# Attention of a macaron block: which engine normalises the first two batches, and the order of copies and exponentials in the first

## The reference, cut to what matters

```python
x = L0_attn_x                                   # (8, 1024, 128) fp32
x = x + 0.5 * _L0_ffn_ref(_layernorm(x), ...)   # feed-forward block with 16 routed experts
x = x + _L0_attn_ref(_layernorm(x), Qw, Kw, Vw) # causal attention, one head, per batch
x = x + 0.5 * _L0_ffn_ref(_layernorm(x), ...)   # the feed-forward block again

def _layernorm(x): return (x - mean) / sqrt(var + 1e-5)      # over the 128 features
def _L0_attn_ref(x, Qw, Kw, Vw):
    scores = (x @ Qw) @ (x @ Kw).T / sqrt(128) + causal_mask
    return softmax(scores) @ (x @ Vw)
```

## Time and profile before

| | us |
|---|---|
| median of 3 runs | 685.28 |
| lowest, highest | 681.53, 686.0 |
| time of the profiled execution | 686.61 |
| its span | 684.8 |
| PE busy | 640.4 (94%) |
| DVE busy | 559.1 (82%) |
| ACT busy | 549.7 (80%) |
| POOL busy | 521.7 (76%) |

### The profile page before, as it was taken

One profiled execution on the slowest core, in us unless ns is written; L12 is line 12 of the kernel. 1 busy time (PEld: TensorE's weight loads), 2 busy tenths in 40 slices (PEclk: granted clock), 3 DMA queues, 4 the chain that ended last, 5 costly groups with the idle time before them and its releaser, 6 DMA issues.

```text
span 684.8 us, 15211 instructions
## 1 busy us (share of the span) xinstructions
PE 640.4 (94%) x3395; PEld 493.8 (72%) x3395; DVE 559.1 (82%) x2576; ACT 549.7 (80%) x1171; POOL 521.7 (76%) x411
## 2 busy tenths in 40 slices
PE   4689999999999997699998998999999999999997
PEld 3457777777777765578776886777777777777775
DVE  5888989989899897767767768779889889898863
ACT  3478879898888874778887786769888898988975
POOL 3378889899998885665655546558899998999975
PEclk9699999999999999999999999999999999999999
DMA  9866677865777650334544435886867878768782
GB/s 245 194 139 128 140 160 151 167 130 129 161 158 165 134 124 1 59 74 76 96 81 78 74 76 96 162 161 123 171 143 159 176 170 174 160 142 187 167 172 76
DMA packets 107801, 92.05 MB, mean 134 GB/s; under 512 B 59488, under 2 KB 73456, under 8 KB 107760
## 3 DMA queue, kind: packets, MB, share of 16 engines
q1 hardware_dynamic: 105552, 91.00, 63.6%
q10 hardware_dynamic: 2208, 0.59, 0.4%
HBM read 72.70 MB, written 5.24 MB: 114 GB/s over the span
## 4 chain that ended last, share of the span: by engine, by line
PE 69%; DVE 13%; ACT 6%; issue 6%; DMA 3%; POOL 2%; SPq 0%; POOLq 0%; ACTq 0%; DVEq 0%
PE psum L1373 18%; PE psum L1374 17%; PE psum L1375 17%; PE psum L1446 3%; DVE w_raw L1246 3%; DMA wb<-scratch 2%; PE psum L1404 2%; PE psum L1458 2%; DVE zn L1272 1%; PE psum L1420 1%; DVE s_sb L1100 1%; PE psum L1412 1%; PE psum L1610 1%; ACT s_sb L759 1%; PE psum L1612 1%
## 5 line engine op out<-in xcount | busy, mean ns | idle before, releaser
L452 POOL TENSOR_TENSOR shared_r<-shared,shared_r 128x512 fp32r<-128x512 f32 x256 | 326.6, 1298 | 57.7 <-ACT shared L642 55.1
L1100 DVE SCALAR_TENSOR_TENSOR s_sb<-psum,wb 128x512 f32<-128x512 f32 x256 | 175.6, 687 | 47.4 <-DMA wb<-scratch 22.4
L641 ACT ACTIVATE shared_r<-s_sb 128x512 fp32r<-128x512 f32 x256 | 160.0, 625 | 46.3 <-DVE s_sb L1100 43.0
L642 ACT ACTIVATE shared<-s_sb 128x512 f32<-128x512 f32 x288 | 177.6, 619 | 20.0 <-DVE s_sb L1100 20.0
L1373 PE MATMUL psum<-x_hi,w_hi 128*128 128x512 f32 x288 | 126.3, 439 | 1.2 <-issue 0.9
L1373 PE MATMUL psum<-shared_r,w_hi 128*128 128x512 f32 x256 | 115.6, 452 | 1.2 <-POOL shared_r L452 1.0
L1375 PE MATMUL psum<-x_hi,w_lo 128*128 128x512 f32 x288 | 114.2, 396 | 0.0
L1374 PE MATMUL psum<-x_lo,w_hi 128*128 128x512 f32 x288 | 114.0, 396 | 0.0
L1374 PE MATMUL psum<-shared_r,w_hi 128*128 128x512 f32 x256 | 101.7, 397 | 0.0
L1375 PE MATMUL psum<-shared_r,w_lo 128*128 128x512 f32 x256 | 101.0, 395 | 0.0
L544 POOL TENSOR_TENSOR shared<-s_sb,shared 128x1024 f16<-128x1024 f32 (+3 forms) x32 | 56.7, 1771 | 44.3 <-ACT shared L572 44.3
(11 more groups left out here) (170 smaller groups left out, 1372.3 us busy)
## 6 DMA issues: line engine op xcount, KB each, us to landing
wb<-scratch SPq DMA_DIRECT2D x128, 512.0 KB, 7.9
out<-x_sb SPq DMA_DIRECT2D x16, 256.0 KB, 9.9
x_sb<-in_L_attn_x SPq DMA_DIRECT2D x4, 256.0 KB, 6.2
scratch<-wT SPq DMA_DIRECT2D x32, 32.0 KB, 1.9
w_raw<-in_L_ffn_W ACTq DMA_DIRECT2D x1, 512.0 KB, 6.0
w_raw<-in_L_ffn_W SPq DMA_DIRECT2D x1, 512.0 KB, 6.6
wb<-shared SPq DMA_TRANSPOSE x32, 4.1
w_raw<-in_L_ffn_Ws ACTq DMA_DIRECT2D x1, 64.0 KB, 8.7
```

Of the source, the lines that this page charges most:

```text
L452: nc.gpsimd.tensor_tensor(g_lo[:, j % RING, :], g_f[:, j % RING, :], g_hi[:, j % RING, :].bitcast(F32), ALU.subtract).then_inc(F.glo_done, 1)
L641: nc.scalar.activation(g_hi[:, j % RING, :], s_sb[:, j % RING, :], ACT.Square)
L642: nc.scalar.activation(g_f[:, j % RING, :], s_sb[:, j % RING, :], ACT.Square).then_inc(F.sq_done, 1)
L1100: ins = nc.vector.scalar_tensor_tensor(s_, h_, 0.0, wb[:, u, c, :], ALU.max, ALU.mult)
```

## The change: what it does

The diff has three parts.

1. DVE's `normalise` is gone. ACT normalises batches 0 and 1 too, two tiles a step: batch 0 at k = 4 to 7 (half 1 first), batch 1 at k = 14 to 17 (half 0 first). ACT needs the bias, so DVE makes `shift(0)` at k = 4 and `shift(1)` at k = 13; the second waits until batch 0 is normalised, since `a_shift` is one buffer.
2. DVE's statistics move: `stats(1, 1)` from k = 4 to 5, `stats(2, 0)` stays at k = 13, `stats(2, 1)` from k = 15 to 14, `mean(2)` from slot 1 of batch 0 to k = 17, and `stats(3, ...)` from slots 1 and 4 of batch 0 to slots 3 and 5.
3. In batch 0 alone, ACT does `exp(0, 0)` and `exp(0, 2)` ahead of the two `z_hi_copy` of batch 1, not behind them. DVE does `z_lo_part(1, 0)` and the last group's residual in slot 1, behind `row_max(0, 1)`, not in slot 0.

```diff
--- before.py
+++ after.py
@@ -772,18 +772,23 @@
                     sc.wait_ge(A.tp_done, HQ * b + SOON.index(t) + 1)
                     copy(pT[:, 0:t + 1, q0:q0 + P], tp_ps[:, 0:(t + 1) * P].rearrange("p (k q) -> p k q", q=P)).then_inc(A.pT_done, 1)
 
-                def normalise(b, half):
-                    sc.wait_ge(A.shift_done, b - 1)
+                def normalise(b, half, tiles=range(HQ)):
+                    sc.wait_ge(A.shift_done, b + 1)
                     tokens_free(sc, b, half)
-                    for t in range(half * HQ, (half + 1) * HQ):
+                    for t in (half * HQ + n for n in tiles):
                         ins = nc.scalar.activation(zn(b, half)[:, t % HQ, :], x_sb[:, b * QT + t, :], ACT.Identity, bias=a_shift[:, t:t + 1],
                                                    scale=a_rstd[:, b % UN, t:t + 1])
-                    ins.then_inc(A.zn_done[half], 1)
+                    if tiles[-1] == HQ - 1:
+                        ins.then_inc(A.zn_done[half], 1)
 
                 def begin(k):
 
                     if k == 3:
                         nc.scalar.activation(warm[:], neg_half[:], ACT.Exp)
+                    if k in (4, 5, 6, 7):
+                        normalise(0, (7 - k) // 2, range(k % 2 * 2, k % 2 * 2 + 2))
+                    if k in (14, 15, 16, 17):
+                        normalise(1, (k - 14) // 2, range(k % 2 * 2, k % 2 * 2 + 2))
                     if k == 8:
                         z_hi_copy(0, 1, misc_ps)
                     if k == 11:
@@ -806,9 +811,11 @@
                                 uT_copy(b - 1, 1)
                             if b > 0 and s == 6:
                                 uT_copy(b - 1, 0)
-                            if b + 1 < B and s in (0, 2):
+                            if b + 1 < B and s in (0, 2) and b > 0:
                                 z_hi_copy(b + 1, s // 2, prep_ps)
                             exp(b, s)
+                            if b == 0 and s in (0, 2):
+                                z_hi_copy(1, s // 2, prep_ps)
                             if s in (5, 6):
                                 pT_copy(b, SOON[s - 5])
                             if b + 1 < B and s in (4, 6):
@@ -1264,15 +1271,6 @@
                     nc.vector.scalar_tensor_tensor(a_shift, a_mv[b % UN][:, :, 0], -1.0, a_rstd[:, b % UN], ALU.mult,
                                                    ALU.mult).then_inc(A.shift_done, 1)
 
-                def normalise(b, half):
-                    v.wait_ge(A.rstd_done, b + 1)
-                    tokens_free(v, b, half)
-                    for t in range(HQ):
-                        tile = half * HQ + t
-                        ins = nc.vector.tensor_scalar(zn(b, half)[:, t, :], x_sb[:, b * QT + tile, :],
-                                                      a_mv[b % UN][:, tile, 0:1], a_rstd[:, b % UN, tile:tile + 1], ALU.subtract, ALU.mult)
-                    ins.then_inc(A.zn_done[half], 1)
-
                 def finish(b, half):
 
                     v.wait_ge(A.exp_done, QT * b + QT - half)
@@ -1294,42 +1292,42 @@
                         stats(0, 1)
                     if k == 2:
                         mean(0)
-                    if k in (3, 4):
-                        stats(1, k - 3)
-                    if k == 5:
-                        normalise(0, 1)
+                    if k == 4:
+                        shift(0)
+                    if k in (3, 5):
+                        stats(1, (k - 3) // 2)
                     if k == 6:
                         mean(1)
-                    if k == 7:
-                        normalise(0, 0)
                     if k == 9:
                         z_lo_part(0, 1, misc_ps)
-                    if k == 10:
-                        normalise(1, 0)
                     if k == 12:
                         z_lo_part(0, 0, u_ps)
-                        normalise(1, 1)
+                    if k == 13:
+                        shift(1)
+                        stats(2, 0)
                     if k == 14:
                         q_lo_part(0, 1, misc_ps)
-                    if k in (13, 15):
-                        stats(2, (k - 13) // 2)
+                        stats(2, 1)
                     if k == 16:
                         q_lo_part(0, 0, u_ps)
+                    if k == 17:
+                        mean(2)
 
                 def run():
                     for b in range(B):
                         for s in range(QT):
                             row_max(b, s)
-                            if b == 0 and s == 0:
+                            if b == 0 and s == 1:
+                                z_lo_part(1, 0, prep_ps)
                                 close_ffn()
                                 v.wait_ge(FF[0].res_done, NG)
-                            if b + 1 < B and s in (0, 2):
+                            if b + 1 < B and s in (0, 2) and (b, s) != (0, 0):
                                 z_lo_part(b + 1, s // 2, prep_ps)
                             if b + 1 < B and s in (5, 7):
                                 q_lo_part(b + 1, (7 - s) // 2, prep_ps)
-                            if b + 2 < B and s == 1:
+                            if 0 < b < B - 2 and s == 1:
                                 mean(b + 2)
-                            if b + 3 < B and s in (1, 4):
+                            if b + 3 < B and s in ((1, 4) if b > 0 else (3, 5)):
                                 stats(b + 3, s // 4)
                             if b + 2 < B and s == 3:
                                 shift(b + 2)
```

## The result

| | before | changed |
|---|---|---|
| median of 11 runs, us | 685.68 | 678.7 |
| lowest, highest | 681.2, 687.84 | 676.38, 679.64 |
| span of the profiled execution | 684.8 | 676.9 |
| mean granted clock | 0.982 | 0.997 |

The ratio is 0.9915, 95% interval 0.9896 to 0.9935: 5.8 us less of 685 (4.5 to 7.1); the two medians alone stand 7.0 apart. The forecast was 678.5, in a range of 675.3 to 682.8. The gain is just short of 1%, on the side that had the larger chance.

What follows compares the result with a forecast made beforehand. DVE's normalising was taken to hold PE before the first score. Gains of 6.4 us by the first row maximum and 7.4 by the fifth, taken as 6.8, bring 685.28 to 678.5 us; range 675.3 to 682.8.

Steps and rivals of the forecast that it cites:

- Who held PE: Before the first score, DVE's four groups of normalising instructions hold PE: about 9.6 us, 5.4 at the median, the rest blocking.
- ACT's run: From 249.14 us ACT does four pairs of squares and eight normalising instructions; zn's halves are ready at 252.9 and 256.4.
- First score: Batch 0's first score on PE starts at 266.1 us instead of 271.37, without a pause, taking 1.5 us instead of 2.7.
- First row maximum: Batch 0's first row maximum on DVE starts at 268.05 us instead of 274.44, 6.4 us gained; `mean(2)` costs 0.4.
- Fifth row maximum: In batch 0, the fifth maximum's exponential starts at 278.25 us instead of 285.69: 7.4 us gained, an extra 1.0.
- Moved whole behind it: From 285.69 us the rest of batch 0 keeps its length and all behind moves with it; gain taken 6.8 us.
- Rival B: PE gaps in batch 0 bring one or two more low-clock spells of 1.2 us: gain 4.4, 680.9 us; chance 0.22.
- Rival C: ACT bounds batch 0; late z copies delay low parts and row maxima; 2.5 to 4 us left, 682; chance 0.16.
- D: Nothing reaches the end because batch 1 starts on another wait (transposing transfers, PE's products): 685 us; chance 0.04.
- E: Moving 16 normalising instructions to ACT costs 0.8 us engine time and takes nothing off the path: 686.1 us; chance 0.02.
- F: PE waits for batch 0's zn at step 8 and runs the tail at low clock: 5 us slower, 690.3; chance 0.04.
- A: The forecast itself, for the whole kernel: gain of 5.8 to 8 us, 677 to 679.5 us; chance 0.52.

Runs made afterwards that it cites:

- the strided kernel: The kernel before, with DVE's normalising instructions reading every second value of two neighbouring tiles; ratio 0.9991 (0.9967 to 1.0014), last gate at 18.51 us.

## Why the prediction was right

- **Who held PE.** DVE, by its L1272. Shown both ways: with the normalising moved to ACT and nothing else the last gate moves from 19.02 to 13.59, and put back as unused work from 13.59 to 19.25.
- **ACT's run.** Forecast 249.14 to 252.9 and 256.4 for the two halves of zn, which is 3.8 and 7.3 behind the anchor. Measured 3.72 (250.60 + 0.86) and 7.35. Steps of streaming instructions, not their durations, were the right price for ACT. For DVE the prediction took durations: L1272 has 0.338 us of duration, but 0.26 from start to start where nothing holds it, so 16 of them are about 4.4 us and not 5.4, more of the 9.6 was blocking than it said, and the move adds about 2 us of plain engine time (0.385 against 0.26), not 0.8.
- **First score.** Forecast 16.96, measured 17.05; without a pause and at full clock.
- **First row maximum.** Forecast 18.91, measured 19.37, a gain of 5.9 instead of 6.4. The missing 0.5 is there already at the last gate (13.25 forecast, 263.0 less a gate of 0.61; 13.59 measured) and the square behind it, and it reaches the low part of the second q whole. The score was ready only 0.16 late, so `mean(2)` cost 0.65 (19.37 against 18.72), not 0.4.
- **Fifth row maximum.** Forecast 7.4 us gained at its exponential, measured 6.66 (36.55 to 29.89). The extra of batch 0's order was put at 1.0 on the way from the first to the fifth; it is 0.7 there (5.93 to 6.66), of which by the estimate above about 0.5 is the order and the rest the tail of the spell that before had at C. Against it stand the 0.65 of `mean(2)`, so the new order as a whole brought about nothing.
- **Moved whole behind it.** D to F: 12.03 before, 11.99 changed. The sum taken, 6.8, stands against 6.7 at F and 5.8 (4.5 to 7.1) in the ratio of the runs. That the forecast time is within 0.2 us of the median is partly luck: the runs of one kernel spread by 3 us and more, and the median of before moved by 0.4 with more runs.
- **Rival B** was half there: the clock fell at the end of batch 0, but it had fallen there before too, so it took nothing from the gain; a spell there is 1.6 us, not 1.2. **Rival C**: DVE's low parts did wait for the late copies (1.16 and 1.66 us idle), but it did not eat the gain. Filling the first wait with `mean(2)` gave 0.65 us at C, moving the second low part behind the fourth maximum 0.45 more by D. **D** did not come. **E**, also the rule of the Trainium skill's page "ScalarE: Activation LUTs", section "Rules for kernel authors", lost: the plain engine time is the smaller part of what an instruction costs on DVE beside a busy POOL. **F**: PE's wait at step 8 was gone.
- **The arithmetic around the forecast** has slips that changed nothing: the lower bound, A's far end of 677 less 1.5, is 675.5 and not 675.3; the upper one is the far end of C's range, not its time of 682; and half and a little more of A's 0.52 is about 0.3, not the 0.43 given to "faster".
- **The shared port.** By the Trainium skill's page "SBUF — State Buffer", section "SBUF: two separate sides", a DVE instruction in a two-port mode, or with two SBUF inputs beside a GpSimd (POOL) instruction that reads SBUF, locks a port pair that the two engines share, and the second to come waits out the first. So it is here: an L1272 that starts beside a subtraction ends with it (1.34 and 1.45 us, against 0.33), and ACT's normalising keeps its 0.385 us a step in the changed kernel. Statistics, with one SBUF input like L1272, were never held. Which instructions run in a two-port mode no run here shows; the strided reading was meant to leave such a mode and was held too. `shift`, with two SBUF inputs, is held as well (1.10 us).

## What to carry to other kernels

Price an instruction on DVE by what POOL does beside it: four small SBUF-to-SBUF operations cost 1.1 us alone (an estimate from 0.33 for one and 0.26 a step) and 2 to 3 beside a stream of subtractions, and what counts is what stands behind them. Work that is needed late (here batch 1) costs most when it stands ahead of the last gates of the phase that is ending. Measure a local change from an anchor just ahead of it: most distances repeated within 0.05 us while the runs spread by several. But look in each profile for what moves them all the same, here the granted clock and a transfer behind the anchor: between them they made an order look worth 0.5 us, and unused products look harmful.

## What the runs showed of the hardware

- In one execution three of four normalising instructions found POOL idle because a transfer was late by 0.8 us more (gate 9 waited 1.91 us, not 1.12), and the last gate came 1.1 us earlier: a later transfer made the stretch shorter.
- A TENSOR_SCALAR 128x128 on DVE beside a POOL subtraction ends when the subtraction ends (1343 and 1450 ns, against 333 and 335 for the next two, which find POOL idle), and the next one, started beside the next subtraction, is held again.
- A TENSOR_SCALAR with stride 2 on its SBUF input is held beside POOL like the contiguous one (maximum 1357 ns, median 342).
- The fall of PE's clock at the end of batch 0 came in some executions and not in others at the same idle times of PE (E to F 5.8 or 4.2 us), and the spell at the first score lasted 3.4 us before and 6.8 in the strided kernel, so a single profile can carry 1.6 us that belongs to no edit.
